# Moving the |W| sums, the split of W and the token transposes of a one-core layer kernel

## The reference, cut to what matters

```python
# layer 0: grouped convolution (9 taps, 4 groups) + a bias, then an int8 product
y = conv(x, w0) + ctx + bias
w_scale = max(|w|) / 127                    # per row
a_scale = max(|y|, axis=-1) / 127           # per token
acc = round(y / a_scale) @ round(w / w_scale).T
x = x + float16(acc * a_scale * w_scale)

# layer 1: a 64x64 channel mix per batch element, then a linear layer with a low-rank part
x2 = agg_w[b] @ x[b] + agg_b[b]
H = x2 @ W.T + b;   z = x2 @ A              # W: L1_ffn_W, 1024 x 1024
weights = soft gate of (H[:, odd rows, :8], z @ LiMEs.T)
x = x + H + (z * (weights @ LiMEs)) @ Bmat * 16 / 32
```

## Time and profile before

| | |
|---|---|
| runs, median (lowest to highest) | 650.16 us (649.19 to 651.15), 3 runs |
| the profiled execution | 650.84 us |
| its span in the trace | 649.0 us |
| PE busy | 622.3 us, 96% |
| DVE busy | 436.7 us, 67% |
| POOL busy | 370.7 us, 57% |
| ACT busy | 337.1 us, 52% |
| DMA | 137.91 MB, mean 212 GB/s |
| granted TensorE clock, mean | 0.984 |
| the step loop, 45 to 311 us | PE busy 255.6 of 266 us |
| behind the loop, 311 to 649 us | PE busy 331.7 of 338 us |

### The profile page before, as it was taken

The page is one execution under the profiler, slowest core; times in us unless marked ns, Lnnn a source line. Parts: engine busy times, 40 slices in busy tenths (PEclk is TensorE's granted clock), DMA queues, the critical chain, the costliest instruction groups (busy, mean ns, idle before and its releaser), DMA issues.

```text
span 649.0 us, 15758 instructions
## 1 busy us (share of the span) xinstructions
PE 622.3 (96%) x6311; PEld 342.7 (53%) x6311; DVE 436.7 (67%) x858; ACT 337.1 (52%) x591; POOL 370.7 (57%) x249
## 2 busy tenths in 40 slices
PE   7789999999999989999999899999999999999997
PEld 5546566666665656666554344444444444444443
DVE  5958999988889887898537785745544433444434
ACT  2858998777877777765513536234323223322100
POOL 3013445556877867872265867785766677656400
PEclk7799999999999999999999899999999999999999
DMA  9978997778777698875237214885554444531103
GB/s 311 370 141 301 363 322 280 255 255 292 280 283 256 230 368 282 299 258 195 69 130 293 97 35 158 308 315 194 191 185 145 161 136 156 194 131 66 65 1 129
DMA packets 46710, 137.91 MB, mean 212 GB/s; under 512 B 13308, under 2 KB 13596, under 8 KB 46465
## 3 DMA queue, kind: packets, MB, share of 16 engines
q1 hardware_dynamic: 41886, 120.13, 53.5%
q10 hardware_dynamic: 4752, 16.78, 7.0%
HBM read 88.61 MB, written 48.28 MB: 211 GB/s over the span
## 4 chain that ended last, share of the span: by engine, by line
PE 72%; DVE 7%; issue 3%; DMA 1%; ACT 1%; POOL 1%; SPq 0%; DVEq 0%; ACTq 0%
PE ps L877 36%; PE ps L686 9%; PE ps L611 8%; PE ps L516 7%; PE ps L649 3%; PE ps L595 2%; PE ps L859 2%; PE ps L580 2%; DVE yb L1392 1%; DMA x_ph<-in_x_phases 1%; DVE f_all L1430 1%; DVE rowmax L1405 1%; PE ps L623 0%; PE ps L669 0%; DVE wst L1474 0%
## 5 line engine op out<-in xcount | busy, mean ns | idle before, releaser
L1220 POOL TENSOR_TENSOR x<-x_in,f_all 128x512 f32<-128x512 f32 x64 | 74.5, 1166 | 105.3 <-DVE f_all L1430 105.3
L611 PE MATMUL ps<-wqT,yq_both 128*128 128x512 bf16 x512 | 120.9, 379 | 1.9 <-ACT wsc_b L934 0.8
L1224 POOL TENSOR_TENSOR x_split<-x_ph,x_split 128x1032 f16<-128x1032 f32 x25 | 53.7, 2148 | 47.8 <-ACT x_split L956 47.8
L983 ACT ACTIVATE yv<-yb,yinv 128x128 f32<-128x128 f32 x256 | 77.8, 387 | 2.7 <-DVE yinv L1421 2.7
L611 PEld LDWEIGHTS ps<-wqT,yq_both 128*128 128x128 bf16 x512 | 45.3, 97 | 49.7 <-issue 1.8
L1264 POOL TENSOR_TENSOR ring<-ring 128x512 f32<-128x512 f32 x52 | 66.0, 1269 | 4.0
L686 PE MATMUL ps<-ffn_wT,ring 128*128 128x512 f16 x288 | 66.4, 386 | 0.0
L1430 DVE SCALAR_TENSOR_TENSOR f_all<-ps,tok_scale,wsc_b 128x512 f16<-128x512 f32 x64 | 47.7, 746 | 19.1 <-PE ps L611 18.7
L516 PE MATMUL ps<-x_split,conv_h 128*64 128x256 f16 (+1 forms) x1248 | 60.0, 274 | 0.4 <-DVE f_all L1430 0.4
L1012 ACT ACTIVATE ring<-ring,pair_inv 128x1024 f32<-128x1024 f32 x26 | 28.4, 1141 | 54.1 <-DVE row_bias L1757 14.6
L516 PEld LDWEIGHTS ps<-x_split,conv_h 128*64 128x64 f16 (+1 forms) x1248 | 48.6, 108 | 9.8 <-issue 5.2
(11 more groups left out here) (337 smaller groups left out, 1210.1 us busy)
## 6 DMA issues: line engine op xcount, KB each, us to landing
x_in<-in_x SPq DMA_DIRECT2D x32, 512.0 KB, 6.7
x_scratch<-x SPq DMA_DIRECT2D x32, 512.0 KB, 4.0
x_ph<-in_x_phases SPq DMA_DIRECT2D x31, 516.0 KB, 5.4
x_scratch<-ring SPq DMA_DIRECT2D x26, 512.0 KB, 5.5
ring<-x_scratch SPq DMA_DIRECT2D x26, 512.0 KB, 4.5
wst<-in_w_nat SPq DMA_DIRECT2D x16, 512.0 KB, 5.5
wst<-in_w_rows SPq DMA_DIRECT2D x12, 512.0 KB, 6.5
x_in<-x_scratch SPq DMA_DIRECT2D x12, 512.0 KB, 4.2
```

The lines of the kernel that those rows point to most:

```text
L611: last = mm(acc_bank(t, h), yqT[:, t % 2, p, :], wqT[:, p, h * HALF:(h + 1) * HALF], start=p == 0, stop=p == PH - 1)
L983: last = A(yv[:, s, :], yb[:, t % 2, s, :], ACT.Copy, scale=yinv[:, s:s + 1], bias=MAGIC)
L1220: g.tensor_tensor(x1[:, t % 2, s], x_in[:, t % 3, s], f16[:, s], ALU.add).then_inc(sem("x1_ready"), 1)
L1224: g.tensor_tensor(x_split[:, (t - SPLIT) % 2, 1, :], phases(t), x_split[:, (t - SPLIT) % 2, 0, :], ALU.subtract).then_inc(sem("xl_ready"), 1)
```

## The change

- **The sums of |W| and of W become one pass.** In every second step from 3 to 17 (`abs_steps`) a natural piece is loaded once (`load_rows`); DVE reduces |W| at the end of the step (`w_abs`), POOL adds the halves and then the quarters (`w_quarters`, adds of 128 x 512 and 128 x 256), and two steps later DVE reduces the 256 that are left (`w_sums`, now ahead of `layer0`). The second load of the natural pieces goes.
- **The split of W comes later, through four buffers.** W_BOUND goes from 12 to 18, W_SPLIT from 14 to 19: `scale_w` in steps 19 to 26, at the end of the step behind `scale_phases`; `w_high` one step later on ACT, `w_low` in POOL step c for the piece of step c. The pieces are staged in wst and x_more. The transpose of the sums (W_TURN) comes in step 21, `row_ends_b` in step 23. The logits start in step 20 in place of 14.
- **The t-pieces:** T_SCALE 23 to 28, T_SUMS 25 to 29; the second pair is scaled in steps 30 and 31; three staging places in place of two.
- **PE** issues `tokens_out(c-1)` ahead of `max_back(c)`.
- **`chan_max`** writes chanmax_rep by a copy of chanmax from SBUF; before it was a maximum with PSUM.
- Some semaphores are merged (zeros_ready, x_scale_ready) with the same conditions.

```diff
-W_ABS, W_BOUND, W_SPLIT, W_SUMS, W_TURN = 3, 12, 14, 21, 29
-T_SCALE, T_SUMS = 23, 25
+W_ABS, W_BOUND, W_SPLIT, W_TURN = 3, 18, 19, 21
+T_SCALE, T_SUMS = 28, 29
...
         def t_stage(q, r):
-            return stage_b[r] if q % 2 == 0 else wst[:, r, :]
+            return stage_b[r] if q % 3 == 0 else x_more[:, r, :] if q == 1 else wst[:, r, :]
+
+        def w_stage(k):
+            return wst[:, k % 2, :] if k % 4 < 2 else x_more[:, k % 2, :]
...
+        abs_steps = tuple(range(W_ABS, W_ABS + 2 * NL, 2))
+        split_loads = {15: 2, 16: 3, 17: 0, 19: 1} | {W_SPLIT - 1 + k: k for k in range(4, NL)}
...
+            def load_rows(k):
+                wait(sp, "w_sum_ready", k - 1)
+                sp.dma_start(wst[:, k % 2, :], w_nat[k * P:(k + 1) * P, :]).then_inc(sem(f"w_loaded{k % 2}"), 16)
+
+            def load_w(k):
+                if k < 2:
+                    sp.wait_ge(sem("w_sum_ready"), NL - 1 + k)
+                elif k >= 4:
+                    sp.wait_ge(sem("w_lo_ready"), k - 3)
+                sp.dma_start(w_stage(k), w_rows[k * P:(k + 1) * P, :]).then_inc(sem(f"w_loaded{k % 4}"), 16)
...
                 if c == T_SCALE - 2:
                     load_t(0)
-                if c == W_SUMS + NL + 1:
+                if c == W_SPLIT + NL + 2:
                     load_t(1)
+                if c == W_SPLIT + NL + 3:
+                    load_t(2)
...
                 max_rows(c)
                 int_product(c - 2, 1, 3, 8)
+                tokens_out(c - 1)
                 max_back(c)
-                tokens_out(c - 1)
...
-                if 0 <= c - W_SPLIT < NL:
-                    w_high(c - W_SPLIT)
-                if 0 <= c - T_SCALE < 2:
-                    t_scale(0, (c - T_SCALE,))
+                if 0 <= c - 1 - W_SPLIT < NL:
+                    w_high(c - 1 - W_SPLIT)
+                if 0 <= c - T_SCALE < 4:
+                    t_scale((c - T_SCALE) // 2, ((c - T_SCALE) % 2,))
...
-            def w_halves(k):
-                pool.wait_ge(sem(f"w_loaded{k % 2}"), 16 * ((2 * NL + k) // 2 + 1))
+            def w_quarters(k):
+                pool.wait_ge(sem("w_abs_ready"), k + 1)
                 src = wst[:, k % 2, :]
-                g.tensor_tensor(src[:, 0:HALF], src[:, 0:HALF], src[:, HALF:L], ALU.add).then_inc(sem("w_half_ready"), 1)
+                for i, n in enumerate((HALF, HALF // 2)):
+                    wait(pool, "w_part_ready", 2 * k + i)
+                    g.tensor_tensor(src[:, 0:n], src[:, 0:n], src[:, n:2 * n], ALU.add).then_inc(sem("w_part_ready"), 1)
...
-                if 0 <= c + 1 - W_SPLIT < NL:
-                    w_low(c + 1 - W_SPLIT)
-                if 0 <= c + 1 - W_SUMS < NL:
-                    w_halves(c + 1 - W_SUMS)
+                if c in abs_steps:
+                    w_quarters(abs_steps.index(c))
+                if 0 <= c - W_SPLIT < NL:
+                    w_low(c - W_SPLIT)
...
                 link(v.tensor_reduce(chanmax[:, :], ps_small[0:8, 0:P].rearrange("p (a c) -> p c a", a=PH), AX.X, ALU.max))
-                v.tensor_tensor(chanmax_rep[:, :, :], ps_small[0:8, 0:P].rearrange("p (a c) -> p a c", a=PH),
-                                chanmax[:, :].unsqueeze(1).to_broadcast([8, PH, CG]), ALU.max).then_inc(sem("chanmax_ready"), 1)
+                v.tensor_copy(chanmax_rep[:, :, :], chanmax[:, :].unsqueeze(1).to_broadcast([8, PH, CG])).then_inc(sem("chanmax_ready"), 1)
...
-                if 0 <= c - W_SPLIT < NL:
-                    scale_w(c - W_SPLIT)
+                if c - 2 in abs_steps:
+                    w_sums(abs_steps.index(c - 2))
                 layer0(c - 2, 0)
                 chan_max(c)
...
-                if 0 <= c - W_ABS < NL:
-                    w_abs(c - W_ABS)
-                if 0 <= c - 1 - W_SUMS < NL:
-                    w_sums(c - 1 - W_SUMS)
+                if c in abs_steps:
+                    w_abs(abs_steps.index(c))
+                if 0 <= c - W_SPLIT < NL:
+                    scale_w(c - W_SPLIT)
```

More of the change, by code:

```diff
@@ L342, in _ @@
             sp.wait_ge(sem("scratch_saved"), 32)
-            sp.wait_ge(sem("mixT_zeroed"), 2)
+            sp.wait_ge(sem("zeros_ready"), 3)
             for h in range(2):
@@ L425, in _ @@
                     load_x(c)
-                if 0 <= c + 1 - W_ABS < NL:
-                    load_w(c + 1 - W_ABS)
-                if 0 <= c + 1 - W_SPLIT < NL:
-                    load_w(NL + c + 1 - W_SPLIT)
-                if 0 <= c + 1 - W_SUMS < NL:
-                    load_w(2 * NL + c + 1 - W_SUMS)
+                if c + 1 in abs_steps:
+                    load_rows(abs_steps.index(c + 1))
+                if c in split_loads:
+                    load_w(split_loads[c])
                 if c == T_SCALE - 2:
                     load_t(0)
-                if c == W_SUMS + NL + 1:
+                if c == W_SPLIT + NL + 2:
                     load_t(1)
+                if c == W_SPLIT + NL + 3:
+                    load_t(2)
                 if c == NT:
                     fetch_x1(0)
-                if c == NT + 2:
-                    load_t(2)
             sp.wait_ge(sem("row_parts_ready"), 4)
@@ L561, in x_total @@
                 wait(pe, "yinv_ready", t - LEAD)
-                wait(pe, "x_bound_ready", splits(t - 1))
+                wait(pe, "x_scale_ready", 3 * splits(t - 1))
                 top = x_sum[:, t:t + 1].bitcast(BF16)[:, 1:2]
@@ L616, in max_rows @@
                 wait(pe, "rowmax_ready", t + 1)
-                wait(pe, "x_bound_ready", splits(min(t + LEAD, NT - 1)) if t >= 3 else 0)
+                wait(pe, "x_scale_ready", 3 * splits(min(t + LEAD, NT - 1)) - 2 if t >= 3 else 0)
                 wait(pe, "bound_ready", len([hi for _, hi in BATCHES if hi <= t]))
@@ L987, in w_high @@
                 act.wait_ge(sem("w_scaled"), k + 1)
-                A(ffn_wT[:, 0, k, :], wst[:, k % 2, :], ACT.Copy).then_inc(sem("w_hi_ready"), 1)
+                A(ffn_wT[:, 0, k, :], w_stage(k), ACT.Copy).then_inc(sem("w_hi_ready"), 1)
             def t_scale(q, rs=(0, 1)):
-                act.wait_ge(sem(f"t_loaded{q % 2}"), 32 * (q // 2 + 1))
+                act.wait_ge(sem(f"t_loaded{q % 3}"), 32 * (q // 3 + 1))
                 if q == 0:
@@ L1019, in x_high @@
                     act.wait_ge(sem("gateT_psum"), 1)
+                if j == 2:
+                    act.wait_ge(sem("t_lo_ready"), 4)
                 if j >= 3:
@@ L1120, in _ @@
             tokens_sb(NT - 1)
-            t_scale(1)
+            t_scale(2)
             high(NT - 2, 0)
@@ L1126, in _ @@
             t_high(1)
-            t_scale(2)
             act.wait_ge(sem("gate_in_ready"), 1)
@@ L1200, in mixT_zero @@
             def mixT_zero(e):
-                g.memset(mixT[e * CH:(e + 1) * CH, :, (1 - e) * CH:(2 - e) * CH], 0.0).then_inc(sem("mixT_zeroed"), 1)
+                g.memset(mixT[e * CH:(e + 1) * CH, :, (1 - e) * CH:(2 - e) * CH], 0.0).then_inc(sem("zeros_ready"), 1)
             g.memset(ones16[:, :], 1.0)
             g.memset(ones_b[:, :], 1.0)
-            g.memset(z_w[:, :, :], 0.0).then_inc(sem("z_w_zeroed"), 1)
-            pool.wait_ge(sem("z_w_zeroed"), 1)
+            g.memset(z_w[:, :, :], 0.0).then_inc(sem("zeros_ready"), 1)
+            pool.wait_ge(sem("zeros_ready"), 1)
             mixT_zero(1)
-            pool.wait_ge(sem("mixT_zeroed"), 1)
+            pool.wait_ge(sem("zeros_ready"), 2)
             mixT_zero(0)
-            pool.wait_ge(sem("mixT_zeroed"), 2)
+            pool.wait_ge(sem("zeros_ready"), 3)
             def add_layer0(t, h):
@@ L1385, in conv_bias @@
                 wait(dve, "yv_ready", t - 1)
-                wait(dve, "x_scale_ready", 2 * splits(t))
+                wait(dve, "x_scale_ready", 3 * splits(t))
                 sets = ps_conv.rearrange("p (s m) -> p s m", m=MB)
@@ L1442, in scale_phases @@
             def scale_phases(t):
[L1443 removed]
+                dve.wait_ge(sem("x_scale_ready"), 3 * splits(t))
                 v.tensor_scalar(phases(t), phases(t), x_up[:, t:t + 1], None, ALU.mult).then_inc(sem("xs_ready"), 1)
```

42 lines of the change are left out of this document (16 added, 26 removed).

## The result

| | before | after |
|---|---|---|
| median of the runs (lowest to highest) | 649.67 us (647.29 to 651.15), 4 runs | 663.56 us (662.19 to 665.01), 4 runs |
| the profiled execution | 650.84 us | 665.01 us |
| its span | 649.0 us | 663.2 us |

The ratio is 1.0218, with a 95% interval of 1.0179 to 1.0256: **slower by 13.9 us**. The forecast was 662.3 (651.5 to 667.0).

The account below looks back on a forecast made before the run. PE was taken as the bound (72% of the chain), DVE and POOL for seven steps after the change. Terms -4.9 + 11.2 + 0.5 + 2.1 + 0.9 + 1.4 + 1.0 = +12.2 us gave 662.3 us on the median's scale, range 651.5 to 667.

Parts of the forecast that it names:

- The mechanism: DVE instructions like `scale_phases` stand still until POOL's ends, then need 0.55 us; POOL gets the turn between two of them.
- Steps 20 to 27: `scale_w` behind `scale_phases` waits for all of `w_low`; DVE and POOL bound seven steps: +11.2 us.
- over 10 us of waits for `rowmax` or `x_bound`: Sign expected in the changed profile: PE's waits for these two in steps 21 to 28 sum to over 10 us.
- The copy: In `chan_max`, the SBUF-to-SBUF copy waits for POOL's first add to end: 0.9 us later in a step.
- The first rival: POOL does not stretch the copy, whose source repeats, but `w_low` still gets its turn: 653.4 us, chance 0.13.
- Steps 14 to 20: `scale_w`, its waits and the logits leave this stretch, so PE runs without waits, 50.6 for 55.5 us: -4.9 us.
- the +1.0: Odd steps 7 to 17 get the copy, `w_sums` and `w_abs` on DVE, about 0.2 us over PE per step pair.
- Steps 4 and 5: Two `w_quarters(0)` adds delay `conv_h` and the `ybias` scaling, so `conv_bias` of step 5 comes later: +1.4 us, between -1.1 and +2.
- Step 2: PE already waits 0.80 us for `chanmax_rep` with POOL in its add; the copy adds +0.9 us.
- Step 28: Step 28 and after: last `w_low` ahead of `t_sum` +0.8, copy +0.9, `w_sums` gone -0.6; half put on PE: +0.5 us.
- Behind the loop: Late `t_sums` on POOL hold `t_high(0)` on ACT and `tokens_sb(31)` behind it, which PE wants at 325.85: +2.1 us.
- At nothing: tokens_out ahead of max_back: On PE, `max_back` comes 0.55 us later, while DVE is busy with the second `f_all`: no cost counted.

Follow-up runs that it names:

- u_wlow: Changed kernel with `w_low` on POOL moved from behind the second `add_layer0` to ahead of the next step's first one: 655.58 us, ratio 1.0081.
- u_swap: Changed kernel with `scale_w` put ahead of `scale_phases` in the same step: 660.70 us, one execution.
- u_copy: Changed kernel with the tensor_tensor with PSUM put back in place of the copy that writes `chanmax_rep`: 651.96 us, ratio 1.0038.
- u_scale: Changed kernel with `scale_w` alone moved back ahead of the first `layer0` of a step: 659.94 us, ratio 1.0157.
- u_tokens: Changed kernel with `tokens_sb` of the last tile ahead of `t_high(0)` on ACT behind the loop: 661.68 us, ratio 1.0191.

## Why the prediction came out

- *The mechanism* held: a DVE instruction from SBUF to SBUF (the reductions aside) waits for POOL's, and between two of them POOL gets its turn. u_wlow (2.62 to 0.74) and u_swap (the two durations exchanged) show it, and `set_mask_s` and `b_ends` are further cases.
- *Steps 20 to 27*: +11.2 forecast, +9.9 measured. The steps from `max_rows` to `max_rows` were 9.6, 10.8, 12.2, 10.8, 9.8, 10.8 and 9.8, for 10.9, 10.9, 12.5, 10.9, 10.0, 10.9 and 10.0; the start of the stretch up to `max_rows` of step 20 was 6.1 for 5.0. I had looked for over 10 us of waits for `rowmax` or `x_bound`; there were 2.8 for x_bound, none for rowmax and 5.9 for yb, 8.7 in this stretch. Behind the longest of them, 2.98 us in step 23, the granted clock was 0.74 from 240.0 to 246.5, a mean over both of its levels, and in the other steps of the stretch 1.00.
- *The copy* is stretched: median 1.00 us against 0.28. The Trainium skill, page "VectorE: DVE Perf Modes", section "What auto-detection actually checks", states the condition that the prediction used (one source and destination in SBUF, outermost dimensions even or equal) for one of VectorE's fast modes; it says nothing there of GpSimd. That it tells which instruction is stretched agrees here with the measured 1.00 and 0.28, with a repeated source too. The first rival, which would have had this term fall, is out. In size the term was too large, 0.9 a step where u_copy shows 0.65 to 0.67 in most.
- *Steps 14 to 20*: -4.9 forecast, -3.4 measured. The step that failed is that I took all six at PE's pace. W_BOUND had moved from 12 to 18, and with it the transposition of `w_max`, which waits for yinv, and the products with `w_top`: steps 18 and 19 took 8.88 and 9.73 where the ones beside them take 7.44 and 9.31. Steps 12 and 13 gave 1.3 back (7.44 and 9.37 for 8.43 and 9.63), which is why steps 6 to 14 came out at -0.15 instead of the +1.0 I had for them. The +1.0 was right in size only: the loss lies almost wholly in step 10 (8.62 for 7.57) and is nearly as large in u_copy (8.44), which has the tensor_tensor again; no run tells why it lies there.
- *Steps 4 and 5*: +1.4 forecast, with a bound of +2; from 3 to 6 it was +5.2 in the profiled execution and +2.1 to +2.4 in those of u_wlow, u_scale, u_swap and u_tokens, whose code there is the same. Even that hides some of it, since `conv(3)` ran at a low clock in the kernel before and at full clock in these. Step 5 alone, at clock 1.00 in both, grew by 3.1, from 11.24 to 14.3. I had the two adds, each with one DVE instruction behind it, but not that the third then runs into `phase_low` (1.99 us), nor what the clock adds. The term was the worst of the sum.
- *Step 2*: +0.9 forecast, PE's wait went from 0.80 to 1.61. *Step 28*: +0.5, measured +0.8, and steps 29 to 31 gave 0.7 back that I had not counted. *Behind the loop*: +2.1; PE's wait was 2.15, and u_tokens, without it, took 1.9 less.
- *"At nothing: tokens_out ahead of max_back"* was wrong as a reading: it is cover for the copy, worth 4 to 7 us in the kernel before. What it is worth without the copy no run shows. It did not upset the sum, because the copy's term counted only what DVE loses, not PE's own wait for `chanmax_rep`, and that wait is what the exchange covers.
- The sum was +12.2; the profiled execution showed +14.2. That the total is within 2 us is partly luck: the steps before 6 cost 3.5 more than forecast and steps 14 to 20 1.5 more, while steps 6 to 14 cost 1.2 less, steps 20 to 27 1.3 less and the rest 0.6 less.
- *Two small slips in the working*: the copy starts 0.15 us behind POOL's first add (124.72 and 124.57), not a quarter; and the first rival's terms give +3.4, not +3.2. Neither moves the forecast.

## What to carry to other kernels

Where VectorE and GpSimd work side by side, count for every VectorE instruction from SBUF to SBUF (here copies, tensor_scalar and scalar_tensor_tensor; the reductions kept their 1.22 us) which GpSimd instruction can be ready when its predecessor ends, whatever its size: eight elements a row paid 2 us. Put such instructions singly, not in rows, or place GpSimd's long ones where VectorE reads PSUM (no run here tests the first of these by itself); moving `w_low` by one call was worth 8 us. And an edit that costs nothing by itself may be what hides another: price it with and without its neighbour.
